# Moved turns of rows, and new orders of work at the passage from attention to the experts

## The reference

```python
mod = (_silu(c) @ wmod).reshape(2, 6, 1, -1)              # sa, ca, ga, sb, cb, gb
h = _layernorm(x) * (1 + ca) + sa
x = x + ga * attention(h, Wqkv, Wout)                     # 16 heads of 64, each query sees the last 128 keys
h = _layernorm(x) * (1 + cb) + sb
# mixture of experts: 8 experts, 2 choices, CAP = 640 rows for each expert and choice
logits = h @ gate_w.T + gate_b
topk_prob, topk_idx = top_k(softmax(logits), 2)
pos = running count of the rows that chose this expert    # dropped from CAP on
hmid = relu(xb @ W1 + b1); yb = hmid @ W2 + b2            # 256 -> 1024 -> 256
x = x + gb * (sum over the choices of prob * yb)
```

## Time and profile before

| | us |
|---|---|
| median of 3 runs | 1151.08 |
| lowest and highest | 1148.5, 1152.78 |
| the profiled execution | 1154.04 |
| its span, first to last instruction | 1152.1 |
| mean granted clock of TensorE | 0.996 of full |

### The profile page before, as it was taken

One profiled execution on the slowest core, in us unless ns is written; L12 is line 12 of the kernel. 1 busy time (PEld: TensorE's weight loads), 2 busy tenths in 40 slices (PEclk: granted clock), 3 DMA queues, 4 the chain that ended last, 5 costly groups with the idle time before them and its releaser, 6 DMA issues.

```text
span 1152.1 us, 25519 instructions
## 1 busy us (share of the span) xinstructions
PE 1096.0 (95%) x9548; PEld 719.4 (62%) x9548; DVE 810.3 (70%) x1739; ACT 679.0 (59%) x1892; POOL 512.0 (44%) x555
## 2 busy tenths in 40 slices
PE   6999999999999999999998898899999999999996
PEld 3455655655655655655655566565867768585865
DVE  6776586586586596586577687697777868686855
ACT  5677476476476476477476564537374654637361
POOL 2243264364364364265255465344344442524342
PEclk9999999999999999999999999999999999999999
DMA  9743000100000000000200001674355373634000
GB/s 332 142 158 127 20 1 20 38 2 25 34 1 24 33 2 29 28 1 25 77 24 33 20 18 48 174 148 73 98 99 140 65 155 82 150 104 87 22 21 9
DMA packets 109715, 77.46 MB, mean 67 GB/s; under 512 B 72842, under 2 KB 100634, under 8 KB 109340
## 3 DMA queue, kind: packets, MB, share of 16 engines
q1 hardware_dynamic: 98844, 54.32, 19.4%
q0 software_dynamic: 10752, 21.54, 6.4%
HBM read 49.99 MB, written 33.78 MB: 73 GB/s over the span
## 4 chain that ended last, share of the span: by engine, by line
PE 78%; issue 6%; POOL 5%; ACT 5%; DVE 4%; DMA 1%; SPq 0%; ACTq 0%; POOLq 0%; DVEq 0%
PE up L1611 17%; PE down L1635 17%; PE gen L565 11%; PE gen L579 6%; PE gen L656 6%; PE score L602 5%; PE pt L613 5%; PE pv L633 5%; PE pv L640 3%; ACT prob L874 2%; POOL probT_split L1382 1%; POOL h L371 1%; POOL probT_split L1384 1%; ACT probT L882 1%; ACT h L842 1%
## 5 line engine op out<-in xcount | busy, mean ns | idle before, releaser
L1661 ACT ACTIVATE hid<-up,b1T 128x512 f16<-128x512 f32 (+1 forms) x192 | 120.8, 629 | 179.0 <-PE up L1611 172.2
L1635 PE MATMUL down<-w,hid 128*128 128x256 f16 x1920 | 214.5, 273 | 5.4 <-issue 3.1
L1382 POOL TENSOR_SCALAR_AFFINE_SELECT probT_split<-probT 128x512 f32<-128x512 f32 x128 | 101.1, 790 | 261.9 <-ACT probT L882 257.8
L1611 PE MATMUL up<-xT,w 128*128 128x512 f16 (+1 forms) x1152 | 212.3, 345 | 3.8 <-issue 2.4
L1635 PEld LDWEIGHTS down<-w,hid 128*128 128x128 f16 x1920 | 186.8, 98 | 32.2 <-issue 4.7
L565 PE MATMUL gen<-hT,big 128*128 128x512 f16 x768 | 185.1, 380 | 7.4 <-ACT h2T L908 4.3
L874 ACT ACTIVATE prob<-score,negmax 128x128 f32<-128x128 f32 x512 | 180.7, 373 | 0.9 <-DVE negmax L1058 0.7
L1611 PEld LDWEIGHTS up<-xT,w 128*128 128x128 f16 x1152 | 113.0, 98 | 98.1 <-issue 4.8
L1757 POOL DMA_INDIRECT out<-y,tail x80 | 85.6, 1070 | 190.4 <-DVE y L1707 176.8
L1677 DVE TENSOR_TENSOR hid<-hid 128x512 f16<-128x512 f32 (+1 forms) x192 | 112.7, 604 | 62.9 <-ACT hid L1662 43.6
L882 ACT ACTIVATE probT<-pt 128x512 f32<-128x512 f32 x128 | 76.8, 600 | 97.1 <-PE pt L613 96.1
(11 more groups left out here) (166 smaller groups left out, 1551.4 us busy)
## 6 DMA issues: line engine op xcount, KB each, us to landing
slot_inputs<-empty_row SPq DMA_DIRECT2D x80, 129.5 KB, 2.5
raw<-slot_inputs SPq DMA_DIRECT2D x28, 320.0 KB
big<-in_L_ffn_W SPq DMA_DIRECT2D x28, 256.0 KB
big<-in_L_ffn_W SPq DMA_DIRECT2D x7, 1024.0 KB
out<-x SPq DMA_DIRECT2D x7, 512.0 KB
x<-in_L_attn_x SPq DMA_DIRECT2D x1, 3072.0 KB, 23.3
kept<-out,tail POOLq DMA_INDIRECT x80
out<-y,tail POOLq DMA_INDIRECT x80
```

Of the source, the lines that this page charges most:

```text
L1382: pool.affine_select(out=probT_split[:, h % 2, :, 1], in_=probT[:, h % 2], pattern=[[0, TILES], [1, P]], compare_op=ALU.is_ge, fill=zero, ...
L1611: mm = pe.matmul(bank, w1[:, par, kd, a, ft * P:(ft + 1) * P], part_rows(e, n, xT[:, par, b * KD + kd, :]), start=(i == 0), stop=(i == 5))
L1635: mm = pe.matmul(down[bank][:, s, :], hid[:, ft, a, t * P:(t + 1) * P], w2[:, par, ft, b, :], start=(i == 0), stop=(i == 3 * FT - 1))
L1661: act.activation(part_rows(e, n, hid[:, ft, 0, :]), bank, ACT.Relu, scale=1 / W_SCALE, bias=bias).then_inc(hid_hi, 1)
```

## The change

It does this, part by part:

- **The turns in the chunks.** On TensorE, in chunks 1 to 6, `route_transposes` moves from behind `transposes` to a place between `scores` and `weighted_values` of the same step (11), and `ln_transposes` of step 5 (chunks 0 to 5) does the same. On ScalarE `route_h2T` moves in front of `copy_probT`; `attn_high` stays in front of both.
- **The modulation of routed rows.** `route_scale` and `route_shift` on GpSimd are gone, as is `norm_rows` for these rows. In their place are `part_scale` (four scalar_tensor_tensor, rows less their mean times the factor) in step 5 and `part_modulate` (four, times the reciprocal deviation plus the shift) in step 6, both on VectorE; the last chunk's early routing has `part_scale` in step 15 instead of 14 and `part_modulate` in 16 instead of 15.
- **The last steps of the last chunk.** `attn_low_part` stands in front of `normalise` from step 15 on.
- **Expert 0.** The turn of round `NC + 1` stands inside the first down product; ScalarE makes two of the four `split_high` around `route_exp`, VectorE two of the four `split_low` in front of the hidden tiles of part 1; `finish` of group 2 stands behind four hidden tiles of part 2.
- **SyncE.** The weights of expert 1 are issued directly behind the first loads of rows, b2B only when part 1 has landed, and the rows of expert 1 only when all parts of expert 0 are turned.

```diff
@@ orders @@
-            ROUTE_AT = {"stats": 4, "rstd": 5, "norm": 6, "scale": 6, "shift": 7, "token": 8, "pack": 9, "low": 9,
+            ROUTE_AT = {"stats": 4, "rstd": 5, "scale": 5, "shift": 6, "token": 8, "pack": 9, "low": 9,
...
-            LAST_AT = {"stats": 4, "rstd": 5, "norm": 5, "scale": 6, "shift": 7, "token": 7, "pack": 8, "low": 8,
+            LAST_AT = {"stats": 4, "rstd": 5, "scale": 5, "shift": 6, "token": 7, "pack": 8, "low": 8,
...
-            EARLY_AT = {"add": 13, "stats": 14, "rstd": 15, "modulate": 15, "pack": 16, "low": 16, "turn": 17, "logits": 18}
+            EARLY_AT = {"add": 13, "stats": 14, "scale": 15, "rstd": 15, "modulate": 16, "pack": 16, "low": 16, "turn": 17, "logits": 18}
@@ TensorE, chunk @@
                             if i < H or not last:
                                 scores(c, i)
+                            if not first and not last and i == at["turn"]:
+                                route_transposes(c)
+                            if i == 5 and c + 2 < NC:
+                                ln_transposes(c, c + 2, "lnT")
...
                             weighted_values(c, i - 4)
...
-                            if not first and i == at["turn"]:
+                            if last and i == at["turn"]:
                                 route_transposes(c)
...
-                            if i == 5 and c + 2 < NC:
-                                ln_transposes(c, c + 2, "lnT")
...
-                        down_product(pe, 0, 0, 0)
-                        route_part_transposes(NC + 1)
+                        down_product(pe, 0, 0, 0, lambda: route_part_transposes(NC + 1))
...
                     for ft in range(FT):
+                        if inside and s == 1 and ft == FT // 2:
+                            inside()
@@ ScalarE @@
                             if not last:
-                                copy_probT(c, i - 2)
                                 if not first and i == at["turn"]:
                                     route_h2T(c)
+                                copy_probT(c, i - 2)
...
                                 route_part_h2T(NC + 1)
+                                split_high(act, 1, 1, 0)
                                 route_exp(NC + 1)
+                                split_high(act, 1, 1, 1)
@@ VectorE @@
                         for stage, unit, there in ((merge, i, new), (invert_sum, i - 1, old), (row_max, i, new),
-                                                   (normalise, i - 1, old)):
+                                                   (attn_low_part, i - 4, last and i > H - 2), (normalise, i - 1, old)):
...
+                            if not first and i == at["scale"]:
+                                part_scale(c)
+                            if not first and i == at["shift"]:
+                                part_modulate(c)
...
                         route_slots(NC + 1)
+                        for i in range(2):
+                            split_low(dve, 1, 1, i)
                         for k_ in range(FT, 2 * FT):
                             hidden_low(dve, 0, k_)
...
-                        for g in range(1, 3):
-                            finish(dve, 0, 0, g)
+                        finish(dve, 0, 0, 1)
                         for k_ in range(2 * FT, UG):
                             hidden_low(dve, 0, k_)
+                            if k_ == 2 * FT + 3:
+                                finish(dve, 0, 0, 2)
@@ GpSimd @@
-                            if not first and i == at["scale"]:
-                                route_scale(pool, c)
-                            if not first and i == at["shift"]:
-                                route_shift(pool, c)
@@ SyncE @@
                     load_first_part(sp, 0)
+                    bank, before = group(LAST, ("v", 1, 3))
+                    sp.wait_ge(gen_full[bank], before + 1)
+                    load_weights(1)
                     sp.wait_ge(x2_ready, 2 * NC)
...
                     load_first_part(sp, 1)
+                    for m in range(K):
+                        sp.wait_ge(raw_first[1][m], 16 * GROUPS)
                     sp.dma_start(b2B[:], b2_in.partition_broadcast(P)).then_inc(b2_loaded, 16)
-                    bank, before = group(LAST, ("v", 1, 3))
-                    sp.wait_ge(gen_full[bank], before + 1)
-                    load_weights(1)
                     sp.wait_ge(sent, 16 * TILES * K * NC)
                     load_first_part(sp, 2)
+                    sp.wait_ge(rows_turned, len(NPART))
                     load_rows(1, 1)
```

More of the change, by code:

```diff
@@ L339, in build @@
                  "k_halo", "v_halo"))
[L340 to L341 removed]
+            x2_ready, r_stat, r_mv, r_var, r_rstd, r_xn, r_h2, r_pack_hi, r_pack = (
+                sem(n) for n in ("x2_ready", "r_stat", "r_mv", "r_var", "r_rstd", "r_xn",
                                  "r_h2", "r_pack_hi", "r_pack"))
@@ L977, in chunk @@
                                 route_part_h2T(NC + 1)
+                                split_high(act, 1, 1, 0)
                                 route_exp(NC + 1)
+                                split_high(act, 1, 1, 1)
                             if k_ == 2 * FT - 1:
-                                for i in range(4):
+                                for i in range(2, 4):
                                     split_high(act, 1, 1, i)
@@ L1238, in chunk @@
                                 keep_v(c, 0)
-                            softmax_step(c, i, last)
                             if last and i == EARLY_AT["logits"]:
                                 route_softmax(NC)
-                            if last:
+                            softmax_step(c, i, last)
+                            if last and i <= H - 2:
                                 attn_low_part(c, i - 4)
@@ L1250, in chunk @@
                             if not first and i == at["stats"]:
-                                dve.wait_ge(x2_ready, 2 * c)
-                                norm_stats(dve, (c - 1) * TILES, stats[1], meanvar[1], r_stat, r_mv, c)
-                            if not first and i == at["norm"]:
-                                norm_rows(dve, (c - 1) * TILES, h2, meanvar[1], rstd[1], r_rstd, r_xn, c)
+                                part_stats(c)
+                            if not first and i == at["scale"]:
+                                part_scale(c)
+                            if not first and i == at["shift"]:
+                                part_modulate(c)
                             if not first and i == at["token"]:
@@ L1262, in chunk @@
                                 part_stats(NC)
+                            if last and i == EARLY_AT["scale"]:
+                                part_scale(NC)
                             if last and i == EARLY_AT["modulate"]:
@@ L1292, in chunk @@
                         part_stats(NC + 1)
+                        part_scale(NC + 1)
                         for k_ in range(2, FT):
@@ L1618, in apart, with down_product @@
                 return e == E - 1 and g == DG - 1
-            def down_product(pe, e, par, g):
+            def down_product(pe, e, par, g, inside=None):
                 n = (par * DG + g) % 2
```

10 lines of the change are left out of this document (3 added, 7 removed).

## The result

The changed kernel takes **1155.94 us** (median of 20 runs, 1152.87 to 1160.35), the kernel before 1151.74 beside it (20 runs, 1148.5 to 1157.88): ratio **1.0039, 95% interval 1.0030 to 1.0048**. It is slower by 4.2 us, where 1145.8 had been forecast; the range ended at 1151.5. The profiled execution of after took 1155.78 us (span 1153.9), at its median.

What follows compares the result with a forecast made beforehand. TensorE was taken as the bound, with stalls to recover in the middle chunks and the turn to the experts. Chunks +0.5 and turn -5.8 gave -5.3 us: 1148.7 profiled, 1145.8 median; own range 1141.5 to 1149.5, full range 1139 to 1151.5.

Steps and rivals of the forecast that it cites:

- Both turns: Middle chunks, steps 5 and 11: moved turns delay attn_high on ScalarE, costing +0.5 and +0.38 us, six times each.
- GpSimd's masks, -4.8: Steps 8 and 9 of six chunks: without GpSimd's modulation the mask waits go, -0.8 us each; bounds -4.8 and -2.
- rival 3: Step 5: VectorE's four part_scale, once over 2.1 us, delay attn_low; 13 us over seven chunks, 1159; chance 0.08.
- The passage, -5.8: Turn from last chunk to experts: -1.3 - 1.9 - 1.7 + 1.6 - 1.2 - 1.3 us.
- that -1.3: Last chunk's end: step 16's product 0.7 us earlier and the clock staying up; -1.3, bounds -0.4 and -2.3.
- The landing (-1.9): Expert 0: rows of part 1 land 2 us earlier, as b2B is issued after them; -1.9 us.
- rival 2: Turn to the experts gives nothing back: DMA queues set the landing, the clock falls as before; 1150; chance 0.22.
- the -1.7 there: Expert 0, part 1: the clock stays up where 18 matmuls ran at half clock; -1.7 us (0 to -1.8).
- The give-back: Expert 0, part 1: two split_low in front of hidden_low make the last hidden tile late; +1.6 us (0 to 2.3).
- The pauses: Expert 0, third down product: half of 2.5 us of pauses without a releaser goes; -1.2 (0 to -2.5).
- the finish order: Expert 0, fourth down product: finish of group 2 behind four hidden tiles removes its stalls; -1.3 us (0 to -1.3).
- The basis: Whole kernel: summed against the profiled execution of 1154.04 us, 3.0 above the median 1151.08, that difference carried over.

Runs made afterwards that it cites:

- e2_mod_back: The changed kernel with the routed rows' modulation back as before (norm_rows on VectorE, multiplication and addition on GpSimd): 1155.42 us, ratio to before 1.0028.
- e4_passage_only: The changed kernel with the moved turns and the modulation in the chunks taken back, leaving the new orders from last chunk to expert 1: 1149.50 us, ratio to before 0.9974.
- e3_round_behind: The changed kernel with ScalarE's attn_high behind the emptying of the turned rows in the two turn steps: 1144.12 us, ratio to before 0.9936.
- e9: The changed kernel with GpSimd's two masks of head 3 in chunk 6 touching 4 columns per tile instead of 128: 1153.72 us in one run.
- e7: The changed kernel with SyncE's weight-load order and the place of two split_high and split_low of expert 1 as before: 1157.88 us, ratio to before 1.0057.
- e8_late_steps_back: The changed kernel with the last chunk's late steps as before (scale step 14, modulate step 15, attn_low_part behind normalising, softmax pass last): 1155.77 us, ratio to before 1.0030.
- e1_turns_back: The changed kernel with both turns of rows in the middle chunks back where they stood, on TensorE and ScalarE: 1149.19 us, ratio to before 0.9984.
- e5: The changed kernel with VectorE taking attn_low in front of normalising in odd steps without a turn: 1145.80 us, ratio to before 0.9948.
- e6: The changed kernel with attn_high behind the turned rows' emptying and attn_low ahead of normalising in odd steps without a turn: 1136.45 us, ratio to before 0.9862.
- e11: e6 with the last chunk's late steps as in the kernel before: 1137.17 us, ratio to before 0.9879.
- e10: e6 with the modulation of the routed rows as in the kernel before: 1138.19 us, ratio to before 0.9884.
- e12: The changed kernel with TensorE's two turns in front of the projection as before and attn_low ahead of normalising in all odd steps: 1139.06 us, ratio to before 0.9887.

## Why the prediction was wrong, point by point

- **Both turns: right, in size too.** The forecast was +0.5 and +0.38 us per chunk, +5.3 in all. The wait in ScalarE's queue was the reason given; the trace shows the idle time in front of `attn_high`, e2_mod_back against e4_passage_only gives +0.91 in chunk 3 and +5.9 by the medians, and e3_round_behind removes both stalls by moving that one instruction.
- **GpSimd's masks, -4.8: the step that failed most.** The masks came early as said, but the gain was 0.34 us per chunk. "Next in line is `attn_low` of step 8, on VectorE, which I place 0.3 us ahead of need" was wrong by some 0.8: I took `part_modulate` as an exchange for `norm_rows` and priced neither of them. It took 2.42 us where `norm_rows` took 1.38. I had the price of the pair beside masks, 1.47, and used it only for step 5, where GpSimd is idle; a step later the masks that I had just freed ran in that very stretch. The forecast stood at the far end of its bounds, and even the near one, -2, was missed: -1.7 in chunks 1 to 5, and +2.4 in chunk 6.
- **Chunk 6: a case left out.** It has no LayerNorm turn, so step 5 is 1.8 us shorter for TensorE while VectorE's work is the same, and in it masks do meet `part_scale`. There rival 3's mechanism held: 2.43 us for four (2.9 was named), a wait of 2.08, and the clock behind it. The threshold that it gave, 2.1 us for the four, doesn't hold there: with 1.66 the wait is still 1.32 (e9). I had argued from chunk 3 for seven chunks, and gave rival 3 a chance of 0.08.
- **The passage, -5.8: near in the trace (-4.96), of which some 3 us are before's long execution, and wrong in its terms.** The product of step 16 came the forecast 0.7 us earlier in ten kernels, but the time went again in front of the next transposes or the turn, so that -1.3 was only 0.1 to 0.6; after's -1.9 there is the clock not falling at step 16 (1.7) and its one pause of 0.94. The landing (-1.9) didn't happen, as rival 2 said: from expert 0's first product to part 1's it is 15.30 us in before, 15.45 in after, and 14.17 in e7 with the old order. The clock did fall in part 1 of after, so the -1.7 there failed. The give-back was 1.16 for 1.6. The pauses went whole, 2.45 us where I had taken half (-1.2), and the finish order gave 1.5 for 1.3.
- **The basis: the other step that failed.** I summed against an execution 3.0 us above the median and carried the difference over, as if every execution had its long passage. By the medians the passage gave 2.4 us (e4_passage_only), not 5. The clock is not what made that execution long: its mean granted clock was 0.996, and that of the 27 runs of before beside e4 was 0.9951. What made its passage some 3 us longer than an average one stays open.
- **What each step is worth in the miss.** By the medians: turns +5.9 for +5.3, modulation +0.5 for -4.8, passage -2.4 for -5.8. The modulation makes 5.3 of the 9.3 us between them, the passage 3.4, the turns 0.6. That the three parts add up to +4.0 is no check, since they were taken off one after the other.

## What to carry to other kernels

An operation that is moved behind another on one engine must be followed into the queue of the engine that answers it: here one copy in front of the turned rows' emptying turned a gain of 2.6 us into a cost of 6.7. When work moves to another engine, price what it replaces as well, in the stretch in which it lands and with what runs beside it there, and look for the one iteration whose steps are shorter. A gain that consists of a clock not falling should be read from medians and from the granted clock of every run, not from one trace.

## What was not expected of the hardware

**The clock doesn't follow the length of a wait alone.** Chunk 6's wait for `attn_low` was the same in five kernels. In after (2.08), e8_late_steps_back (2.10) and e3_round_behind (2.09) the granted clock fell to 1.2 GHz behind it; in e1_turns_back (2.09) and e7_sync_back (2.09) it stayed at 2.4. TensorE of e1_turns_back:

```profile
573.58 0.65 PE L624 MATMUL pv<-probT_split,v 128*64 128x256 f32 x4 [2.09 <-DVE attn L1071]
...
575.09 1.46 PE L556 MATMUL gen<-hT,big 128*128 128x512 f16 x6
```

It costs some 1.2 us there: chunk 6 took 78.13 us in after and 76.95 in e7_sync_back with the same work. In the passage every trace has at least one fall, and only its place changes: at step 16 in before, e2, e5, e6, e7, e9 and e11; in the first up part in e1, e3, e4, e5, e10, e11 and e12 (7 us for 5.4); in part 1 in before, after, e2, e8 and e9; and in e7 also in the down products behind part 1.

**Masks lengthen operations with two inputs on VectorE**: in chunk 6 by 0.77 us for two masks, as e9 showed by itself. Four such operations took 1.66 us alone, 2.04 beside one mask (e5, chunk 6), 2.43 beside two.
